# Three key tiles in place of two turned by VectorE, for 36 of 128 heads, in memory that the second residual gave up

## What is computed

```python
q, k, v = heads(x @ Wq + bq), heads(ctx @ Wk + bk), heads(ctx @ Wv + bv)   # 16 heads of 64
att = softmax((q / sqrt(8)) @ k.T, axis=-1)                                # 512 queries x 512 keys
x = layernorm(x + (att @ v) @ Wo + bo)
```

## Time and profile before

| | |
|---|---|
| median of 3 runs | 1879.73 us (1879.31 to 1880.47) |
| profiled execution | 1877.74 us |
| its span, first to last instruction | 1875.7 us |
| granted TensorE clock, mean | 0.997 |
| busy TensorE, VectorE, ScalarE, GpSimd | 98%, 84%, 62%, 56% |

### The profile page before, as it was taken

The page is one execution under the profiler, slowest core; times in us unless marked ns, Lnnn a source line. Parts: engine busy times, 40 slices in busy tenths (PEclk is TensorE's granted clock), DMA queues, the critical chain, the costliest instruction groups (busy, mean ns, idle before and its releaser), DMA issues.

```text
span 1875.7 us, 28846 instructions
## 1 busy us (share of the span) xinstructions
PE 1847.2 (98%) x8863; PEld 1524.0 (81%) x8863; DVE 1573.4 (84%) x3386; ACT 1160.8 (62%) x2461; POOL 1042.6 (56%) x1108
## 2 busy tenths in 40 slices
PE   9999999989999999999999999999999999999998
PEld 8888888768888888888888888888888877678887
DVE  6676666788888998989889888998989899958887
ACT  5544554466777776776767777776777777622221
POOL 2322234245567676656656566666655667746773
PEclk9999999999999999999999999999999999999999
DMA  5777787975759686585786858676586776522121
GB/s 224 275 291 279 281 309 272 316 258 182 249 163 316 207 270 221 158 263 155 256 259 180 279 154 272 185 228 221 155 266 178 252 221 218 153 78 90 58 79 68
DMA packets 200920, 400.39 MB, mean 213 GB/s; under 512 B 18112, under 2 KB 82112, under 8 KB 198592
## 3 DMA queue, kind: packets, MB, share of 16 engines
q1 hardware_dynamic: 164720, 329.08, 53.7%
q10 hardware_dynamic: 36048, 69.48, 11.3%
HBM read 211.31 MB, written 88.08 MB: 160 GB/s over the span
## 4 chain that ended last, share of the span: by engine, by line
PE 90%; DVE 6%; ACT 1%; DMA 1%; POOL 1%; issue 1%; ACTq 0%; POOLq 0%; DVEq 0%
PE a_proj L1419 17%; PE a_turned L1419 17%; PE a_av L1458 11%; PE a_score L1432 11%; PE a_proj L48 9%; PE a_proj L1842 5%; PE a_av L1842 5%; PE a_score L48 3%; PE a_av L48 3%; PE a_turned L1442 3%; PE a_proj L1442 3%; DVE all_negmax L1232 1%; DMA all_second_buffer<-x1T_scratch 1%; DVE c_squares L1288 1%; PE a_score L1817 1%
## 5 line engine op out<-in xcount | busy, mean ns | idle before, releaser
L1020 POOL TENSOR_SCALAR c_prob<-c_prob,all_rden 128x512 f32<-128x512 f32 x512 | 352.1, 695 | 497.4 <-DVE all_rden L1238 497.4
L1098 ACT ACTIVATE c_prob<-a_score,all_negmax 128x512 f32<-128x512 f32 x512 | 347.9, 685 | 193.4 <-DVE all_negmax L1232 190.3
L1232 DVE TENSOR_REDUCE all_negmax<-a_score 128x1 f32<-128x512 f32 x512 | 328.9, 684 | 94.3 <-PE a_score L1432 94.2
L1027 POOL TENSOR_TENSOR c_landing<-c_landing,c_flip_hi 128x512 fp32r<-128x512 f32 x250 | 318.1, 1294 | 7.4 <-ACT c_flip_hi L1148 7.4
L1288 DVE STREAM_TRANSPOSE c_squares<-c_prob 128x256 f32<-128x256 f32 x500 | 292.2, 622 | 2.7 <-POOL c_prob L1020 2.5
L1432 PE MATMUL a_score<-c_ks,c_qs 128*128 128x512 f32 x1024 | 277.1, 392 | 7.7 <-ACT c_prob L1098 7.0
L1432 PEld LDWEIGHTS a_score<-c_ks,c_qs 128*128 128x128 f32 x1024 | 190.1, 188 | 54.2 <-ACT c_prob L1098 7.2
L1458 PE MATMUL a_av<-c_pt,c_vs 128*128 128x512 f32 x512 | 158.9, 392 | 0.0
L343 POOL TENSOR_SCALAR s_prob<-s_prob,s_rden 128x512 f32<-128x512 f32 x32 | 22.2, 693 | 227.6 <-DVE s_rden L515 227.6
L1148 ACT CAST c_flip_hi<-c_landing 128x512 fp32r<-128x512 f32 x250 | 143.3, 625 | 2.2 <-issue 2.1
L1419 PE MATMUL a_turned<-all_second_buffer,c_wq 128*128 128x512 f32 x552 | 140.3, 403 | 3.9 <-DMA all_second_buffer<-x1T_scratch 3.9
(11 more groups left out here) (230 smaller groups left out, 4053.1 us busy)
## 6 DMA issues: line engine op xcount, KB each, us to landing
c_landing<-c_squares SPq DMA_DIRECT2D x500, 128.0 KB, 2.7
c_wk<-wk_scratch SPq DMA_DIRECT2D x64, 512.0 KB, 3.9
c_wq<-wq_scratch SPq DMA_DIRECT2D x64, 512.0 KB, 4.6
c_ks<-c_ks SPq DMA_DIRECT2D x128, 256.0 KB, 3.6
all_first_buffer<-ctxT_scratch ACTq DMA_DIRECT2D x60, 512.0 KB, 7.9
all_second_buffer<-x1T_scratch ACTq DMA_DIRECT2D x60, 512.0 KB, 6.9
ctxT_scratch<-s_csp SPq DMA_DIRECT2D x8, 2048.0 KB, 7.4
c_y<-y_steps_scratch SPq DMA_DIRECT2D x16, 1024.0 KB, 5.6
```

The costliest lines, as they stand in the source:

```text
L1020: nc.gpsimd.tensor_scalar(prob[:, n % 2, i, :], prob[:, n % 2, i, :], rden[:, n % 2, i:i + 1], 1.0, ALU.mult, ALU.mult).then_inc(p_ready, 1)
L1027: nc.gpsimd.tensor_tensor(whole, as_f32(whole), by_square(as_f32(flip_hi_part[:, k, :])), ALU.subtract).then_inc(flip_lo, 1)
L1098: nc.scalar.activation(prob[:, n % 2, i, :], spsum[:, i % 2, :], ACT.Exp, bias=negmax[:, n % 2, i:i + 1], scale=1.0, accum_out=den[:, n % ...
L1232: nc.vector.tensor_reduce(negmax[:, n % 2, i:i + 1], spsum[:, i % 2, :], AX.X, ALU.max, negate=True).then_inc(smax, 1)
```

## The change

THIRD holds the odd heads of groups 4 to 12, 36 heads. For these `flip` takes three key tiles (columns 128 to 511) in place of two, `turned_in` drops the turn of key tile 1, and `send_squares` sends 192 KB in place of 128 KB in each of its four DMAs. The third tile's high part is copied and subtracted in step 2n+2, one step ahead of the other two (`third_head`). Squares, landing and high part of these heads have buffers of their own, laid where `x2` was: `x2` is now allocated by each of the three parts of the program, at the same address, and cross-attention puts its new buffers there, between the weights' split (VectorE waits once for their stores) and the load of the second residual (SyncE waits once for all products of the groups before 13).

```diff
                                                for n in ("first", "second", "third"))
         self.wv_loaded, self.c_loaded = sc.sem("wv_loaded"), [sc.sem(f"c_loaded{k}") for k in range(D // P)]
         self.x_loaded = sc.sem("x1T_loaded")
-        self.x2, self.bo = sc.sb("x2", [P, 2, T, D]), sc.sb("bo", [P, D])
+        self.bo = sc.sb("bo", [P, D])
         self.bo_loaded = sc.sem("bo_loaded")
         self.y_loaded = [sc.sem(f"y2_loaded{u}") for u in range(2)]
         self.passed = sc.sem("passed")
...
     sp, pool, act, dve, pe = nc.sync, nc.gpsimd, nc.scalar, nc.vector, nc.tensor
     proj, spsum, tpsum, opsum = banks
     A, WV, qp = held.first, held.second, held.third
+    held.x2 = sc.sb("x2", [P, 2, T, D])
     upper, ms = held.x2[:, 0, :, :], held.x2[:, 1, :, :]
     x1t = sc.sb("x1t", [P, 2, K, S], F32R)
...
     WHOLE = (0, 1, HH * GROUPS - 1)
     FLIPS = {head: n + 1 for n, head in enumerate(h for h in range(HH * GROUPS) if h not in WHOLE)}
+
+    THIRD = [h for g in range(4, GROUPS - 3) for h in range(HH * g + 1, HH * g + HH, 2)]
+
+    def flipped_of(head):
+
+        return T - TURNED + (head in THIRD)
+
+    PARTS, parts = {}, 0
+    for head in FLIPS:
+        PARTS[head], parts = parts, parts + flipped_of(head)
+
     LANDINGS = {head: sum(h % 2 == head % 2 for h in FLIPS if h <= head) for head in FLIPS}
     def turned_in(g, step):
         n, half = divmod(step, 2)
+        if HH * g + n in THIRD and half:
+            return []
         return [(g, T * n + k) for k in ((2 * half, 2 * half + 1) if HH * g + n in WHOLE else (half,))]
     def valued_in(g, step):
...
         n = step // 2 - 1
         return None if step % 2 == 0 or HH * g + n not in FLIPS else (g, n) if n >= 0 else (g - 1, HH - 1)
+    def third_head(g, step):
+
+        n = step // 2 - 1
+        return None if step % 2 or HH * g + n not in THIRD else (g, n) if n >= 0 else (g - 1, HH - 1)
+
     def head_done(g, step):
         n = step // 2 - 2
...
     sp, pool, act, dve, pe = nc.sync, nc.gpsimd, nc.scalar, nc.vector, nc.tensor
     WV, cp, xp = held.third, held.first, held.second
+
+    third_squares, third_landing = (sc.sb("third_squares", [P, SQUARES, 3, T, Q]),
+                                    sc.sb("third_landing", [P, SQUARES, 3, T * Q], F32R))
+    third_hi_part = sc.sb("third_hi", [P, S], F32R)
+    sc.sb("third_unused", [P, S])
     y, osum = sc.sb("y", [P, T, D]), sc.sb("osum", [P, 2, S])
     squares_out = [sc.sb("squares0", [P, SQUARES, FLIPPED, T, Q])]
     ks, qs = sc.sb("ks", [P, 2, 2, 2, S], F32R), sc.sb("qs", [P, 2, 2, S], F32R)
...
         return bank.rearrange("p (a i q) -> p i a q", a=SQUARES, i=T)
+    def squares_of(head):
+        return third_squares[:, :, :, :, :] if head in THIRD else squares_out[head % 2][:, :, :, :, :]
+
+    def landing_of(head):
+        return third_landing[:, :, :, :] if head in THIRD else landing[:, head % 2, :, :, :]
+
+    def hi_of(k):
+
+        return flip_hi_part[:, k - TURNED, :] if k >= TURNED else third_hi_part[:, :]
+
     def op_of(g):
         return op if g < GROUPS - 1 else held.first
...
         sp.wait_ge(flipped, T * FLIPS[head])
         wait(sp, av_mm, T * (head - 1))
         for a in range(SQUARES):
-            sp.dma_start(as_f32(landing[:, head % 2, a, :, :]).rearrange("p k n -> p (k n)"),
-                         squares_out[head % 2][a * Q:(a + 1) * Q].rearrange("p m k i q -> p (m k i q)")).then_inc(
+            sp.dma_start(as_f32(landing_of(head)[:, a, :, :]).rearrange("p k n -> p (k n)"),
+                         squares_of(head)[a * Q:(a + 1) * Q].rearrange("p m k i q -> p (m k i q)")).then_inc(
                              landed[head % 2], 16)
     def sync_weights():
...
             sync_second()
         if g in WEIGHT_GROUPS and 9 <= step < 9 + K:
             me.after.sync_split(WEIGHT_GROUPS.index(g), step - 9)
+        if step == 5 and g == GROUPS - 3:
+            sp.wait_ge(av_mm, TILES * g)
         if step == 5 and g in (GROUPS - 3, GROUPS - 2):
             me.after.sync_first(g - GROUPS + 3)
...
     def flip_lo_tile(g, n, k):
         head = HH * g + n
-        pool.wait_ge(flip_hi, FLIPPED * (FLIPS[head] - 1) + k + 1)
-        whole = landing[:, head % 2, :, k, :]
-        nc.gpsimd.tensor_tensor(whole, as_f32(whole), by_square(as_f32(flip_hi_part[:, k, :])),
-                                ALU.subtract).then_inc(flip_lo, 1)
+        f = k - T + flipped_of(head)
+        pool.wait_ge(flip_hi, PARTS[head] + f + 1)
+        whole = landing_of(head)[:, :, f, :]
+        nc.gpsimd.tensor_tensor(whole, as_f32(whole), by_square(as_f32(hi_of(k))), ALU.subtract).then_inc(flip_lo, 1)
     def split_out(g, j):
         pool.wait_ge(o_sum, HH * g + 2 * j + 2)
...
             if step == 3 and g:
                 split_out(g - 1, PAIRS - 1)
             if landed_head(g, step):
-                for k in range(FLIPPED):
+                for k in range(TURNED, T):
                     flip_lo_tile(*landed_head(g, step), k)
+            if third_head(g, step):
+                flip_lo_tile(*third_head(g, step), TURNED - 1)
             for tile in ahead(g, step):
                 norm_tile(*tile)
             if step == 0 and g:
...
     def pt_part(g, t, m):
         n, k = divmod(t, T)
-        if k < TURNED:
+        if (g, t) in TURN and k < TURNED:
             return pt[:, k, m, :]
-        return by_square(flip_hi_part[:, k - TURNED, :]) if m == HI else landing[:, n % 2, :, k - TURNED, :]
+        head = HH * g + n
+        return by_square(hi_of(k)) if m == HI else landing_of(head)[:, :, k - T + flipped_of(head), :]
     def like(part, bank):
...
     def flip_hi_tile(g, n, k):
         head = HH * g + n
+        f = k - T + flipped_of(head)
         act.wait_ge(landed[head % 2], 16 * SQUARES * LANDINGS[head])
-        wait(act, av_mm, T * (head - 1) + TURNED + k + 1)
-        nc.scalar.copy(by_square(flip_hi_part[:, k, :]), as_f32(landing[:, head % 2, :, k, :])).then_inc(flip_hi, 1)
+        wait(act, av_mm, T * (head - 1) + k + 1)
+        nc.scalar.copy(by_square(hi_of(k)), as_f32(landing_of(head)[:, :, f, :])).then_inc(flip_hi, 1)
     def out_part(g, n):
...
         for step in range(STEPS):
             item, tiles, head = SCHEDULE[g][step], ahead(g, step), head_done(g, step)
             if landed_head(g, step):
-                for k in range(FLIPPED):
+                for k in range(TURNED, T):
                     flip_hi_tile(*landed_head(g, step), k)
+            if third_head(g, step):
+                flip_hi_tile(*third_head(g, step), TURNED - 1)
             if item and item[0] != "O":
                 proj_hi_part(item)
             for tile in tiles:
...
         dve.wait_ge(p_ready, TILES * g + t + 1)
         if i == 0:
             wait(dve, landed[head % 2], 16 * SQUARES * (LANDINGS[head] - 1))
-        nc.vector.transpose(squares_out[head % 2][:, :, :, i, :].rearrange("p m k q -> p k m q"),
-                            prob[:, n % 2, i, TURNED * P:].rearrange("p (k j m) -> p k m j", k=FLIPPED, m=SQUARES)).then_inc(
-                                flipped, 1)
+            if head == THIRD[0]:
+                dve.wait_ge(me.after.f_stored, 64 * T)
+        count = flipped_of(head)
+        nc.vector.transpose(squares_of(head)[:, :, :, i, :].rearrange("p m k q -> p k m q"),
+                            prob[:, n % 2, i, (T - count) * P:].rearrange("p (k j m) -> p k m j", k=count,
+                                                                          m=SQUARES)).then_inc(flipped, 1)
     def o_second(g, n):
         head = HH * g + n
...
         if (g, t) in TURN:
             pe.wait_ge(pt_lo, TURN[g, t])
         else:
-            pe.wait_ge(flip_lo, FLIPPED * (FLIPS[head] - 1) + k - TURNED + 1)
+            pe.wait_ge(flip_lo, PARTS[head] + k - T + flipped_of(head) + 1)
         for m in (HI, LO):
             ins = nc.tensor.matmul(opsum[:, n % 2, :], vs[:, g % 2, k, n, :], pt_part(g, t, m),
                                    start=(k == 0 and m == HI), stop=(k == T - 1 and m == LO))
...
     PAD = 8
     assert NB % RING == 0 and T == 4 and K == 4 and NG < PAD
     sp, pool, act, dve, pe = nc.sync, nc.gpsimd, nc.scalar, nc.vector, nc.tensor
+    held.x2 = sc.sb("x2", [P, 2, T, D])
     x2, W = held.x2, [held.second, held.third]
     sc.sb("over_y", [P, 16, 256])
...
     WEIGHT_STEPS = 1 + T + 2 + 2
     norm2, norm3 = held.norm2, Norm(sc, T, D, held.passed, "norm3")
     me = Part()
-    me.x2_lo, me.weights = x2_lo, 2
+    me.x2_lo, me.f_stored, me.weights = x2_lo, f_stored, 2
     def batches(step):
```

## The result

The changed kernel takes 1889.96 us (median of 7 runs) against 1879.31 us of the kernel before on the same chip: ratio 1.0058, 95% interval 1.0045 to 1.0070. It is slower by some 10.7 us, outside the predicted range of 1873.0 to 1888.5 and on the side that rival 4 had. One of the seven runs took 6221 us at a granted clock of 0.308 and is left out of the ratio; the other six lie between 1884.6 and 1892.7 us, median 1889.46. The profiled execution took 1888.96 us, span 1887.0.

A forecast was written before the change was run, and what follows sets the result against it. TensorE, busy 98% of the span, was taken to bound the kernel. Terms -15.8 + 9.5 + 5.7 + 1.0 = +0.4 gave 1878.1 us on the profiled execution, 1880.1 for the median; range 1873 to 1888.5.

The forecast's parts named there:

- rival 4: At step 8 head 3's squares hold ScalarE, delaying step 9's scores: 1889 us, 1898 at full growth; chance 0.27.
- What bounds the kernel: TensorE, busy 98% of the span, waits 0.4 us in 900, so every piece of its work removed is time.
- what goes: Each of 36 heads loses one key tile's turn, four transposes on TensorE, 0.44 us each: 15.8 us off the path.
- x: Extra VectorE time of a 128x384 flip over a 128x256 one: 0.23 us taken, bounds 0.13 and 0.31.
- Rival 2: VectorE's longer flips run at one column a cycle: 3.6 us under the forecast, 1876.5, or 1870.2 with rival 1; chance 0.10.
- First term: Step 4: head 1's longer flips delay GpSimd's normalisations, so TensorE's transposes wait 1.06 us a group, 9.5 us in nine.
- Second term: Step 12: Q0+ waits for the last x1T load, delayed by head 3's bytes and wanted sooner: 5.7 us, bounds 0 and 9.
- Third term: Step 8: head 3's squares land late for ScalarE's earlier copy, fitting by 0.2 us; 1 us added over nine groups.
- Rival 1: The DMA waits at the loads don't come, leaving -15.8 + 9.5 = -6.3: 1873.4 us; chance 0.16.

The follow-up runs named there:

- the first run: The changed kernel with the third tile's squares not sent and zeros in its landing, against the kernel before: 1874.91 us, ratio 0.9981.

## Why the prediction was wrong

**What bounds the kernel, what goes:** right. TensorE had no slack, and 36 turns are worth 36 x 0.49 = 17.6 us (15.8 forecast; the chain's 0.44 us is the transposes, and of the rest most is that the eleven matmuls behind them start 224 to 236 ns apart in place of 227, which adds up to 0.04). The runs with head 7 and with heads 2 and 7 got all of it within their intervals.

**x:** right, 0.23 us. Rival 2 falls. Two sizes now give the rate, (853-623)/128 = 1.80 ns a column, and 163 ns that don't scale. The Trainium skill (Vector Engine (DVE) Microarchitecture Reference, section 3.8) has the transpose front end sustain one element per cycle per lane; the prediction worked out 0.13 us for 128 columns from it, as an estimate. They took 0.23 us here, so this trace doesn't agree, and the measurement decides.

**First term, step 4:** right in place and cause, 0.83 us a group for 1.06. Part of it came at another waiter: GpSimd's late split_out held the last quarter of the output projection of step 4 (0.31 us), then its flipped tile the products (0.52); the turn behind them had no wait of its own left. Head 1 alone reproduced it.

**Second term, the loads:** the step that failed, by its size. The mechanism was the forecast's (late x1T at step 12, from head 3's bytes and the earlier demand), but it cost 2.18 us a group, 19.6 us, for 5.7. "256 KB at 357 GB/s is 0.73 us ... 0.65 is taken" is the term: the last x1T piece landed 2.3 us later, counted from step 6's scores, and head 3's bytes alone moved it by 1.7. Put into the forecast's own sum, 2.3 and the 0.98 us of two turns in place of 0.65 and 0.88 give 18.9 us. The 0.65 was bytes over a mean rate, with nothing measured behind it. A bound of 9 us "if the bytes cost twice as much" was too narrow for the same reason (its own sum gives 10.1). The context's last piece was not looked at: its slack at V0+ was 1.4 us before (landing at 17.99, wanted at 19.38 us from step 6's scores), and the same bytes used it up. It adds nothing to the 2.18 while x1T is later still, but it is what remains, 0.92 us a group, when the store of y is moved.

**Third term and rival 4, ScalarE held:** ScalarE was held at the copy, head 3's in every group, and its exponentials of step 8 began 0.8 to 1.5 us later than before; but the scores of step 9 never waited for it: step 8 stayed at 5.47 us. The 1 us set aside was in no wait at the scores. Rival 4's time, 1889, is what was measured, but not by its mechanism, so that is luck: its condition, squares that land later than some 3.9 us after step 8's scores, was met in no group (2.0 to 2.8, and 1.1 to 2.8 before), and the first run kept the early copy and its wait, and lost the loss. Its chance stood for the wrong thing. (Two figures of the rivals are off by their own working: 1898 at the full growth should be some 1902, and 1870.2 for rivals 1 and 2 together 1869.8.)

**Rival 1** (the DMA waits don't come) was the opposite of the truth for head 3 and true for heads 5 and 7.

Sum with measured terms, on the profile: -17.6 + 7.5 + 19.6 = +9.5. The span grew by 11.3; from group 4 to 13 it grew by 9.8, and the rest lies outside the nine groups, where the change does nothing; it isn't explained.

## What to carry to other kernels

Work taken off a full engine must be paid for with a resource that is idle at that moment: ask at which step the replacement's instructions and bytes fall, not what share of the whole they are. The same edit was worth its full 0.49 us for heads 2 and 7, minus 0.36 for head 1 and minus 1.2 us for head 3. In a stretch in which DMA is full, read the slack of every load that lands in it, and don't take bytes over the mean rate for the price of extra bytes: here the landing moved by over twice that. And where the chain of waits runs through a held queue, lay the times beside the same event in the kernel before, before that queue is blamed. When two waits follow each other, ask what the second would be without the first before adding them up as two causes.

## What the runs showed of the hardware that was not expected

256 KB from SBUF to SBUF in the full stretch moved another queue's landing by 1.7 us (some 0.5 either way), 2.3 times the 0.73 us at the stretch's mean rate. A part of it shows in the packets, worked out from the traces of head 3 with 128 and with 192 KB in each DMA, between the scores of steps 6 and 11. Head 3's squares are 512 packets a group in that stretch with either size; the packets of 1.0 KB there took 47 ns in the mean, those of 1.5 KB 69 ns, which over sixteen engines is 0.7 us more. The loads' packets of 2 KB took 99.9 ns in place of 97.8, some 2,300 of them a group, another 0.3. What makes the other 0.7 us is open.

Outside that stretch the same squares are slower: over the whole of 690 to 1410 us of the changed kernel the 1.5 KB packets of all four heads took 86 ns in the mean, 66 in the stretch. No run here shows why.
